# A cross-attention and gated feed-forward layer: feed-forward in two passes with the gated values in DRAM, and an attention that streams x by batch and transposes by DMA

## What is computed

```
Q = layernorm(x) @ Wq.T + bq ; K = ctx @ Wk.T + bk
x = x + softmax(Q K.T / sqrt(1024)) @ ctx
Wg, Wu (3584 x 1024), Wd (1024 x 3584): 4-bit codes, 16 values, times one scale per block of 64
n = layernorm(x)
out = x + (silu(n @ Wg.T) * (n @ Wu.T)) @ Wd.T
```

## Time and profile before

| | us |
|---|---|
| median of the runs | 2295.63 |
| the profiled execution, its own time | 2300.16 |
| its span | 2298.3 |
| TensorE busy | 2185.6 |
| DVE busy | 1639.9 |
| ACT busy | 1227.8 |
| POOL busy | 406.6 |

### The profile page before, as it was taken

One profiled execution on the slowest core, in us unless ns is written; L12 is line 12 of the kernel. 1 busy time (PEld: TensorE's weight loads), 2 busy tenths in 40 slices (PEclk: granted clock), 3 DMA queues, 4 the chain that ended last, 5 costly groups with the idle time before them and its releaser, 6 DMA issues.

```text
span 2298.3 us, 33430 instructions
## 1 busy us (share of the span) xinstructions
PE 2185.6 (95%) x10934; PEld 1092.0 (48%) x10934; DVE 1639.9 (71%) x2501; ACT 1227.8 (53%) x2130; POOL 406.6 (18%) x384
## 2 busy tenths in 40 slices
PE   8869899879899999999999999999999999999998
PEld 3357777644334444444444444444444444444443
DVE  7665455677886867768686868777686868687644
ACT  4754444546755556555656555555556565555420
POOL 0021221401212121121212121111212121212100
PEclk9979999999999999999999999999999999999999
DMA  9011010012322221222222222212222222222103
GB/s 318 19 28 38 19 37 18 23 28 48 70 49 53 49 50 44 56 55 51 52 51 51 49 50 51 51 42 56 57 51 51 51 52 48 53 49 51 42 5 151
DMA packets 243501, 124.67 MB, mean 54 GB/s; under 512 B 191088, under 2 KB 219760, under 8 KB 243312
## 3 DMA queue, kind: packets, MB, share of 16 engines
q1 hardware_dynamic: 240800, 121.57, 21.5%
q10 hardware_dynamic: 2512, 0.79, 0.1%
HBM read 69.90 MB, written 8.39 MB: 34 GB/s over the span
## 4 chain that ended last, share of the span: by engine, by line
PE 71%; DVE 3%; issue 2%; ACT 2%; DVEq 0%; DMA 0%; ACTq 0%; POOLq 0%; POOL 0%
PE ps L1469 46%; PE ps L1488 24%; DVE w L211 2%; DVE act_buf L1371 1%; ACT halves L221 1%; ACT sq L198 1%; DVE y L1380 0%; PE ps L1457 0%; DVE xT L1359 0%; ACT act_buf L1318 0%; DVE halves L227 0%; DMA q<-in_L_ffn_up_q 0%; DVE h L1354 0%; ACT w L193 0%; ACT xT L1292 0%
## 5 line engine op out<-in xcount | busy, mean ns | idle before, releaser
L1469 PE MATMUL ps<-xT,wgu 128*128 128x512 f16 x5376 | 1171.3, 380 | 16.0 <-DVE xT L1359 6.7
L211 DVE SCALAR_TENSOR_TENSOR w<-sq,w 128x512 f32<-128x512 f32 x1176 | 834.6, 710 | 195.9 <-ACT sq L198 118.2
L198 ACT ACTIVATE sq<-q 128x512 f32<-128x512 int32 x1176 | 714.5, 626 | 428.8 <-DVE w L211 424.9
L1469 PEld LDWEIGHTS ps<-xT,wgu 128*128 128x128 f16 x5376 | 526.3, 98 | 649.5 <-issue 15.0
L1488 PE MATMUL ps<-wd,h 128*128 128x512 f16 x2688 | 594.0, 381 | 24.5 <-DVE y L1380 21.7
L1488 PEld LDWEIGHTS ps<-wd,h 128*128 128x128 f16 x2688 | 256.9, 98 | 359.5 <-DVE y L1380 88.1
L1380 DVE SCALAR_TENSOR_TENSOR y<-ps,y_out,y 128x512 f32<-128x512 f32 x448 | 331.4, 740 | 40.2 <-PE ps L1488 40.2
L227 DVE SCALAR_TENSOR_TENSOR halves<-w,halves 128x512 f16<-128x512 f32 x168 | 173.9, 1035 | 141.8 <-ACT halves L221 141.8
L802 PE MATMUL ps<-wgu,xT 128*128 128x256 f16 x1536 | 181.9, 280 | 16.1 <-ACT RT L854 11.2
L1324 ACT CAST h<-act_buf 128x512 f16<-128x512 f32 x112 | 69.1, 617 | 218.2 <-DVE act_buf L1371 218.2
L802 PEld LDWEIGHTS ps<-wgu,xT 128*128 128x128 f16 x1536 | 153.1, 100 | 40.3 <-ACT RT L854 12.7
(11 more groups left out here) (154 smaller groups left out, 952.4 us busy)
## 6 DMA issues: line engine op xcount, KB each, us to landing
q<-in_L_ffn_down_q SPq DMA_DIRECT2D x56, 256.0 KB, 3.2
q<-in_L_ffn_up_q SPq DMA_DIRECT2D x55, 256.0 KB, 2.8
q<-in_L_ffn_gate_q SPq DMA_DIRECT2D x54, 256.0 KB, 2.6
y<-in_x SPq DMA_DIRECT2D x4, 2048.0 KB, 20.1
xT<-in_ctx SPq DMA_DIRECT2D x8, 1024.0 KB, 5.0
out<-y SPq DMA_DIRECT2D x3, 2048.0 KB, 6.6
xT<-in_L_xattn_Wq SPq DMA_DIRECT2D x8, 512.0 KB, 10.6
wk<-in_L_xattn_Wk SPq DMA_DIRECT2D x16, 256.0 KB, 11.0
```

The costliest lines, as they stand in the source:

```text
L198: nc.scalar.activation(un.sq[:, (i - even) % 2, :], un.q[:, ring, :], ACT.Square, bias=b, scale=a).then_inc(un.s_act, 1)
L211: nc.vector.scalar_tensor_tensor(out=un.w[:, slot, :], in0=un.sq[:, (i + 1 - even) % 2, :], scalar=FACTORS[i][2], in1=un.w[:, slot, :], op ...
L1469: last = nc.tensor.matmul(ps[:, 2 + 2 * mat + n % 2, :], un.wgu[:, odd, mat, k // 4, a, k % 4, :], t.xT[:, n, c, k, :], start=k == 0 and j ...
```

## The change

1. The feed-forward becomes two blocks. **hidden_layer** does all gate and up products, chunk by chunk (28 chunks of four groups), and stores the gated values (hi and lo) in DRAM (`hs`); it also makes the down units and stores them in DRAM (`wds`). **down_layer** then loads both again and accumulates the sum over all 28 chunks in PSUM: 112 steps of 24 matmuls on 8 banks, with 32 evictions in all instead of 448. x after attention lies in DRAM (`ys`), and its normalised, transposed parts too (`xs`).
2. **split_lo moves from DVE to POOL.** The rings `sq` and `halves` have three places, `wgu` holds four chunks. No unit is made in prepare; attend makes one per batch, hidden_layer the other 160.
3. **attend** loads x by batch. x, the keys and the new x (of two batches before) are normalised or scaled, split (hi on ACT, lo on POOL) and transposed by DMA (`turn_tile`, `turn_keys`, 128 x 2048 f16 each), not by TensorE. Normalised tiles go through a ring `xr` of two places in the order of `TILES`: x of the next batch, then y of two batches before.
4. The maximum over partitions for the next batch (`key_all`) moves from the end of a step into it, between the sixth and the seventh subtraction of R on POOL.
5. All loops are written out; waits are on constants.

```diff
+def units_during(c):
+    return [UNIT_OF[unit] for unit in UNITS[EARLY_UNITS:] if unit[0] == (c if unit[1][0] == 2 else c + EARLY_CHUNKS)]
...
-def split_lo(nc, dve, un, u, slot, ring):
-    dve.wait_ge(un.s_whi, u + 1)
-    nc.vector.scalar_tensor_tensor(out=un.halves[:, ring, 1, :], in0=un.w[:, slot, :], scalar=1.0, in1=un.halves[:, ring, 0, :],
-                                   op0=ALU.mult, op1=ALU.subtract).then_inc(un.s_wlo, 1)
+def split_lo(nc, pool, un, u):
+    pool.wait_ge(un.s_whi, u + 1)
+    nc.gpsimd.tensor_tensor(un.halves[:, u % T_RING, 1, :], un.w[:, u % W_RING, :], un.halves[:, u % T_RING, 0, :],
+                            ALU.subtract).then_inc(un.s_wlo, 1)
...
+TILES = [("x", 0, 0), ("x", 0, 1)]
+for _b in range(BATCH):
+    if _b + 1 < BATCH:
+        TILES += [("x", _b + 1, 0), ("x", _b + 1, 1)]
+    if _b >= 2:
+        TILES += [("y", _b - 2, 0), ("y", _b - 2, 1)]
...
+def normalise(nc, dve, at, r, tile, col):
+    wait(dve, at.s_tlo, r - 1)
+    nc.vector.tensor_scalar(at.xr[:, r % 2, :], tile, at.mv[:, col, 0:1], at.rstd[:, col:col + 1],
+                            ALU.subtract, ALU.mult).then_inc(at.s_norm, 1)
...
+def key_all(nc, pool, at, b):
+    pool.wait_ge(at.s_kmax, b + 1)
+    nc.gpsimd.tensor_tensor(at.spare[:, :], at.kmax[:, :], at.kmax[:, :], ALU.subtract)
+    nc.gpsimd.partition_all_reduce(at.kall[:, :], at.kmax[:, :], P, bass.bass_isa.ReduceOp.max).then_inc(at.s_kall, 1)
...
+                    for o in range(KT):
+                        r_lo(b, o)
+                        if b >= 1 and o < TB:
+                            keys_lo(nc, pool, at, b, o)
+                        if o == 2:
+                            scale_unit(nc, pool, un, t, b)
+                        if more and o == 5:
+                            tile_lo(nc, pool, at, TILE_OF["x", b + 1, 0])
+                            key_all(nc, pool, at, b + 1)
+                        if more and o == 6:
+                            tile_lo(nc, pool, at, TILE_OF["x", b + 1, 1])
+                    if b >= 2:
+                        for i in range(TB):
+                            tile_lo(nc, pool, at, TILE_OF["y", b - 2, i])
+                    split_lo(nc, pool, un, b)
...
+                    for n in range(TB):
+                        if old:
+                            normalise(nc, dve, at, TILE_OF["y", b - 2, n], y_tile(b - 2, n), TB + n)
+                        for _, _ in zip(range(2), todo):
+                            pass
+                    if b > 0:
+                        residual(b - 1)
+                    softmax(b)
...
+                            wait(pe, s_y, ATT * b + n - 1)
...
+                        wait(pe, s_h, g - PS_RING + 1)
+                        for mat, done in ((0, s_g), (1, s_u)):
+                            for k in range(KT):
+                                for j, (a, b) in enumerate(PARTS):
+                                    last = nc.tensor.matmul(ps[:, 2 * (g % PS_RING) + mat, :], un.wgu[:, c % WC_RING, mat, k // 4, a, k % 4, :],
+                                                            xT[:, n, :, b, k, :], start=k == 0 and j == 0, stop=k == KT - 1 and j == 2)
...
+                            last = nc.tensor.matmul(ps[:, j, :], h[:, m % H_RING, j // BT, a, tok],
+                                                    wd[:, half, c, b].rearrange("p k d -> p (k d)"),
+                                                    start=c == 0 and n == 0, stop=c == CH - 1 and n == len(PARTS) - 1)
```

More of the change, by code:

```diff
@@ L89, in block_of @@
[L89 to L106, removed]
+Q_RING, SQ_RING, W_RING, T_RING = 3, 3, 3, 3
+WC_RING = 4
+Y_RING = 4
+ROW_BANK, COL_BANK = 4, 3
+R_BANKS = 4
+PARTS = ((0, 0), (0, 1), (1, 0))
@@ new lines, with unit_order @@
+GATE_UP = [(0, 0), (0, 1), (1, 0), (1, 1)]
+EARLY_CHUNKS = 2
+def unit_order():
+    units = [(c, kind) for c in range(EARLY_CHUNKS) for kind in GATE_UP]
+    for c in range(CH):
+        ahead = [(c + EARLY_CHUNKS, kind) for kind in GATE_UP] if c + EARLY_CHUNKS < CH else []
+        down = [(c, (2, 0)), (c, (2, 1))]
+        units += ahead[:2] + down[:1] + ahead[2:] + down[1:]
+    return units
+UNITS = unit_order()
+UNIT_OF = {unit: u for u, unit in enumerate(UNITS)}
+EARLY_UNITS = EARLY_CHUNKS * len(GATE_UP)
@@ L109, in wait, with ring_count @@
+def units_during(c):
+    return [UNIT_OF[unit] for unit in UNITS[EARLY_UNITS:] if unit[0] == (c if unit[1][0] == 2 else c + EARLY_CHUNKS)]
 def wait(eng, sem, count):
-    if not isinstance(count, int) or count > 0:
+    if count > 0:
         eng.wait_ge(sem, count)
[L115 to L128, removed]
+def ring_count(n, ring):
+    return 16 * (n // ring + 1)
@@ L231, in turn_unit @@
-def turn_unit(nc, sp, un, u, ring, dst):
-    sp.wait_ge(un.s_wlo, u + 1)
[L234 to L243, removed]
+    wait(act, un.s_turned[u % T_RING], 16 * (u // T_RING))
+    nc.scalar.copy(un.halves[:, u % T_RING, 0, :], un.w[:, u % W_RING, :]).then_inc(un.s_whi, 1)
@@ L1129, in feed_forward, with schedule, hidden_layer @@
-def feed_forward(nc, t, un):
+                row_sums(BATCH - 1)
+                residual(BATCH - 1)
+GROUPS = CH * NBLK
+def schedule(c):
+    units = units_during(c)
+    halves = [(u, part) for u in units for part in range(2)]
+    for n in range(NBLK):
+        yield n, halves[n * len(halves) // NBLK:(n + 1) * len(halves) // NBLK]
+def hidden_layer(nc, t, un):
     with ExitStack() as st:
@@ new lines, in _ @@
+                dve.wait_ge(s_yl, 16)
+                for r in range(BT):
+                    last = moments(nc, lt, yl[:, r, :], r)
+                link(last)
+                scales_of(nc, lt, slice(0, BT), link)
+                for r in range(BT):
+                    normalise(nc, dve, lt, r, yl[:, r, :], r)
+                for c in range(CH):
+                    for n, halves in schedule(c):
+                        for u, part in halves:
+                            if part == 0:
+                                steps = factors(nc, dve, un, u)
+                            for _, _ in zip(range((3, 4)[part]), steps):
+                                pass
+                        hidden(NBLK * c + n - 1)
```

1462 lines of the change are left out of this document (633 added, 829 removed).

## The result

The changed kernel takes 2351.89 us (median of 4 runs, 2347.0 to 2353.11) against 2295.7 in the same session (2295.46 to 2299.48): 1.0237 times as long, 95% interval 1.0219 to 1.0255. The prediction was 2355.5, slower. The profiled execution has a span of 2350.4, where the sum said 2358.

A forecast was written before the change was run, and what follows sets the result against it. TensorE bound the old kernel; DVE would bind pass one. Attend to 540, first factor 580, pass one to 1757, between passes to 1772, pass two to 2353, plus 5: span 2358, predicted time 2355.5 us, range 2275 to 2405.

The forecast's parts named there:

- R starts: End of prepare: R's first start moves from 138.7 to 126 us, between 120 and 139.
- Attend: Steps of 43, 45, five times 56, then 34 and 12: sum 414 us, TensorE leaving at 540.
- the second program change: In attend, POOL's next ordinary instruction comes 6.9 us after the reduction's end.
- To pass one: Between attend and the feed-forward: storing the last x and reading transposed x takes 14 us, bounds 8 and 25.
- Pass one: Gate and up products: DVE's pace of 42.9 us per chunk binds, 26 chunks from 580 to 1695, end 1757.
- Between the passes: From gate and up products to down products: 13 us, plus 2 for the restart, to 1772.
- Pass two: Down products: 2688 matmuls at 0.216 take 580.5 us, to 2353, strided operands priced at nothing.
- Rival two: Attend: no program change around the reduction, 88 us less, 2267.5; chance 0.12.
- Rival one: Pass one stays TensorE's at 41.5 us per chunk, total 2313.5; chance 0.22.
- rival three: Pass one: every POOL instruction costs DVE its whole length, 47.8 us per chunk, total 2483; chance 0.07.
- Rival four: Attention costs little more than now, 45 us a step, total 2300, no difference; chance 0.08.
- R's slow restart (+1.6): Attend: 24 matmuls of R took 4.32 us after an idle 3.9 us, against 2.7: +1.6.

The follow-up runs named there:

- e1_reduce_later: Changed kernel with the reduction over partitions moved behind the last subtraction of R and both x tiles on POOL: 2328.83 us.
- e2_residual: Changed kernel with DVE's residual of the batch before put ahead of the key scales and y tiles in attend: 2329.72 us.
- e4_split_dve: Changed kernel with the lo half of pass one's weight units moved back from POOL to DVE: 2324.3 us.
- e9_sp_order: Changed kernel with residual first, lo half on DVE, maximum by matmul in attend, and SP's loads of x and keys asked for earlier: 2245.12 us.
- e5_both: Changed kernel with both edits, residual first in attend and pass one's lo half on DVE: 2307.81 us.

## Why the prediction was right

By its own steps:

- **R starts** at 118.9 (126, bounds 120 to 139): outside its bounds, by 1 us. No run shows which term of prepare was worth more than I gave it. These 7 us and 5 of attend's steps made pass one begin 12 early; its chunks gave 7 back, and the places between, smaller than taken, make the sum 8 us too long. That errors of 12 and of 7 us have opposite signs is luck.
- **Attend.** Batch 0 44.6 (43), batch 1 44.2 (45), batches 2 to 6 276.3 together (280), the last with its product 44.5 (46). Sum 409.6 (414), its end at 528.4 (540). The chain inside a long step, from the start of R at 374.44: key maximum ends at 22.8 (23.2), reduction at 30.2 (29.7), POOL's next ordinary instruction at 37.4 (36.6), tile of x ends at 40.2 (39.4), first residual at 45.3 (46.6), two products 4.2 (4.1), next R at 54.8 (56). This is the mechanism of the sum, link by link. In batch 0 it is not: there TensorE waits 13.1 us in the scores for POOL's subtraction of R, which stands behind the reduction (the row at 155.00), and then goes on without a wait for the turned tile of x that I had named as the bound. That 43 came so near is luck. The price of the second program change was the row of 6.90, and 7.20 was measured.
- **To pass one** 12.5 (14). The first factor is at 568.1 (580), 27 behind TensorE's start (26).
- **Pass one.** 43.17 per chunk (42.9). From the first factor at 568.06 to the last wait of TensorE at 1690.49 are 1122.4 us, which is 26 x 43.17, as the sum built it. The six groups left are TensorE's, 62.3 (62).
- **One wait was not in the sum and cost nothing**: TensorE runs through four groups until 585.0 and stands 5.08 us, since DVE is then the bound already and the pass counts from its first factor.
- **Between the passes** 12.1 (15). **Pass two** 581.8 (580.5), strided operands cost nothing that shows: 0.216 each, and it never waits for a load behind its first. From its end to the end of the span 3.7 (5).

Rival two priced the program changes at 88 us, to give 2267.5 if they were not there. They are there, so its condition is false. The run without a reduction took 2268.2, but the price agrees by luck: from R's first start to the end of attend 74 us went, not 88 (the five long steps gave 54.5 and not 80, batches 0 and 1 gave 18 and not 8), and 10.7 more went ahead of R, with a reduction that this rival did not count. Rival one (pass one stays TensorE's) fell by 1.7 us per chunk, rival three by the factor of 952 ns and the run with the extra reader. Rival four had taken steps of 45, which only kernels without the reduction have.

What I got wrong lies behind the prediction, in what an edit would win. Four of my expectations (e1_reduce_later, e2_residual, e4_split_dve, e9_sp_order) were 10 to 31 us too low: they priced the wait removed and not what stood next (the later reduction, SP's late load of x, DVE's own work).

## What to carry to other kernels

Here the one POOL instruction of another program, which computes for 0.38 us, cost 6 us before and 7 behind it. Look at what stands in POOL's queue behind it, in whose rings, and which engine waits for those. The maximum over partitions of one column was cheaper as one f32 matmul of the broadcast column with an identity and a maximum of the row: 1 us instead of 13.6.

Moving work from a busy DVE to an idle POOL was no gain where both read two operands from SBUF: DVE was 1 us per chunk slower for having given away one of eight instructions per unit.

When a wait is taken out, ask each queue what is late next, SP's order of transfers first, before putting a number on it.

## What the runs showed that I had not expected

- A fill by POOL that reads nothing leaves DVE's factors alone (958 ns against 952) and yet cost 0.20 us per unit, most of it in waits for a silu that ACT does late; why it is late is open.
- Of TensorE's clock: in the step that starts at 374.44 the granted clock was 1.00 from 380 to 396, while TensorE worked, and 0.50 (1.2 of 2.4 GHz) from 404 to 419, in the wait of 21 us. It was still 0.50 from 419.8 to 423, and 1.00 from 424. The 12 matmuls behind the wait took 4.38 us, where the 12 ahead of it took 2.75. The mean granted clock is 0.962 for the changed kernel and 0.983 before. The estimate from R's slow restart (+1.6) fitted, but it comes with every such wait: where the waits are short, in the last kernel, the granted clock is 0.979.
- Two executions with the same preparation can differ by 3 us before attend begins: R first starts at 117.4 in e2_residual and at 120.6 in e5_both.
